# A message-passing layer on one NeuronCore: irregular edge groups moved to a second pass, and another order of TensorE's step

## The reference

```python
h = relu(layernorm(x))
emb = edge_attr_128 @ W_edge + b_edge            # 20000 x 512
msg = relu(h[src] + emb)
h2 = (1 + eps) * h + segment_sum(msg, dst, N)
h2 = gelu(layer_norm(h2 @ W1 + b1, g1, be1))     # 512 -> 1024
h2 = gelu(layer_norm(h2 @ W2 + b2, g2, be2))     # 1024 -> 512
h3 = layer_norm(h + h2, gA, bA)
out = x + layer_norm(h3 + gelu(h3 @ M1) @ M2, gB, bB)
```

## Time and profile before

| quantity | value |
|---|---|
| times of three runs | 535.83, 531.12, 531.4 us; median 531.4 |
| span of the profiled execution | 528.1 us |
| busy PE | 471.7 us, 89% |
| busy PEld | 344.2 us, 65% |
| busy DVE | 393.5 us, 75% |
| busy ACT | 309.2 us, 59% |
| busy POOL | 278.4 us, 53% |
| DMA | 85.53 MB, mean 162 GB/s |

### The profile page before, as it was taken

The page is one execution under the profiler, slowest core; times in us unless marked ns, Lnnn a source line. Parts: engine busy times, 40 slices in busy tenths (PEclk is TensorE's granted clock), DMA queues, the critical chain, the costliest instruction groups (busy, mean ns, idle before and its releaser), DMA issues.

```text
span 528.1 us, 7261 instructions
## 1 busy us (share of the span) xinstructions
PE 471.7 (89%) x1930; PEld 344.2 (65%) x1930; DVE 393.5 (75%) x564; ACT 309.2 (59%) x584; POOL 278.4 (53%) x295
## 2 busy tenths in 40 slices
PE   1397996979996999789987999999999999999994
PEld 0034664646664656446655888888888889888884
DVE  7953995869894889679796577777999866672575
ACT  5643785858874877769793555555666656013000
POOL 5575775767875777667600345533554463330252
PEclk9999998998998999999999999999999999999998
DMA  8956887776786777667604733243551132130122
GB/s 268 345 169 192 305 263 229 231 227 189 248 248 180 207 233 231 185 200 227 188 11 142 260 99 118 82 160 99 159 160 40 61 93 68 40 119 2 41 80 81
DMA packets 31717, 85.53 MB, mean 162 GB/s; under 512 B 4880, under 2 KB 5216, under 8 KB 31648
## 3 DMA queue, kind: packets, MB, share of 16 engines
q0 software_dynamic: 12688, 41.17, 26.7%
q1 hardware_dynamic: 18960, 43.52, 24.7%
HBM read 72.08 MB, written 5.25 MB: 146 GB/s over the span
## 4 chain that ended last, share of the span: by engine, by line
PE 43%; DVE 15%; ACT 14%; issue 11%; ACTq 6%; another core or an unknown queue 3%; POOL 3%; DMA 3%; POOLq 0%; DVEq 0%; SPq 0%
PE ps_u L1288 8%; PE ps_u L1290 8%; PE ps_u L1289 8%; DVE msg_lo L1090 5%; DVE z L1084 5%; ACT apart L690 5%; ACT msg_hi L774 5%; PE ps_t L1290 4%; PE ps_t L1289 4%; PE ps_t L1288 4%; PE ps_t L1462 2%; PE ps_u L1305 2%; DMA w_raw<-in_W 2%; PE ps_t L1323 2%
## 5 line engine op out<-in xcount | busy, mean ns | idle before, releaser
L578 POOL DMA_INDIRECT rows<-gather_table,src_idx x153 | 166.4, 1087 | 66.7 <-issue 43.8
L774 ACT ACTIVATE msg_hi<-z 128x1024 fp32r<-128x1024 f32 (+1 forms) x79 | 82.6, 1046 | 33.4 <-DVE z L1084 22.0
L584 POOL TENSOR_TENSOR var_eps<-mv,eps_t 128x1 f32<-128x1 f32 x40 | 21.5, 536 | 144.0 <-ACT squares L832 85.6
L1090 DVE SCALAR_TENSOR_TENSOR msg_lo<-z,msg_hi 128x1024 fp32r<-128x1024 f32 (+1 forms) x79 | 95.4, 1209 | 0.6 <-ACT msg_hi L774 0.6
L1084 DVE TENSOR_TENSOR z<-ps_u,rows 128x1024 f32<-128x1024 f32 (+1 forms) x53 | 64.3, 1213 | 40.0 <-remote 24.2
L1305 PE MATMUL ps_u<-we_raw,attr_raw 128*128 128x512 f32 x130 | 69.4, 636 | 19.0 <-DVE z L1084 18.4
L1323 PE MATMUL ps_t<-msg_lo,onehot 128*128 128x512 f32 x149 | 64.9, 436 | 2.2 <-ACT onehot L696 1.2
L1288 PE MATMUL ps_u<-w_hi,lhs_lo 128*128 128x512 f32 x160 | 64.5, 403 | 1.5 <-DVE lhs_lo L1132 1.5
L1290 PE MATMUL ps_u<-w_hi,lhs_hi 128*128 128x512 f32 x160 | 62.6, 391 | 0.0
L1289 PE MATMUL ps_u<-w_lo,lhs_hi 128*128 128x512 f32 x160 | 62.3, 389 | 0.0
L1323 PE MATMUL ps_t<-msg_hi,onehot 128*128 128x512 f32 x149 | 59.1, 397 | 0.8 <-issue 0.8
(11 more groups left out here) (179 smaller groups left out, 1015.1 us busy)
## 6 DMA issues: line engine op xcount, KB each, us to landing
attr_raw<-in_attr_t SPq DMA_DIRECT2D x20, 512.0 KB
w_raw<-in_W SPq DMA_DIRECT2D x24, 256.0 KB, 2.8
tile_in<-mid SPq DMA_DIRECT2D x10, 512.0 KB, 3.5
res<-in_x SPq DMA_DIRECT2D x20, 256.0 KB, 2.7
xin<-in_x SPq DMA_DIRECT2D x5, 512.0 KB, 5.6
out<-work SPq DMA_DIRECT2D x10, 256.0 KB, 2.0
rows<-gather_table,src_idx POOLq DMA_INDIRECT x153
gather_table<-tab SPq DMA_DIRECT2D x4, 512.0 KB
```

Source lines behind the costliest of these rows:

```text
L578: g.indirect_dma_start(rows[:, group.r, e % TPG, :], None, gather_table[:, :], bass.IndirectOffsetOnAxis(src_idx[:, e:e + 1].bitcast(u32), ...
L774: a.activation(pair(msg_hi, g, p), summed(g, p), ACT.Relu).then_inc(msg_hi_done, 1)
L1090: v.scalar_tensor_tensor(pair(msg_lo, g, p), summed(g, p), 0.0, pair(msg_hi, g, p).bitcast(f32), ALU.max, ALU.subtract).then_inc(msg_lo_do ...
```

## The change

- **TensorE's step** makes both products first (second pair of g+1, first pair of g+2), then handles an event of group g-1, then scatters both pairs of g-1 with `onehot`, event or not.
- **A plain event** no longer needs a pair with only one window. `old_nodes` scatters into the old window the second pair if bit 4 of the word says that it has edges there, and always the first pair; then TensorE waits for `prefilled` and both pairs are scattered into the new window.
- **Any other event** is a `switch` on ScalarE: close the window before, prefill the group's last one. The group's edges in its last window are scattered as always; those in its other windows are left to a second pass behind the edge stage.
- **The second pass** (`late_windows`) runs on all five engines over all groups, and within a group over the windows left out, one at a time: SyncE loads the attributes, GpSimd gathers the rows, TensorE makes the products, VectorE and ScalarE the messages and a selection, TensorE the sum, VectorE adds it to `acc`. A count in the plan says how many such windows there are; where it is 0 each engine skips the pass. In these inputs it is 0.
- `one_by_one`, `general`, `select_extra` and their tiles and semaphores go; SyncE and GpSimd now wait for the plan before they read the count; the plan's words change.

```diff
-EVENT, COUNTS, SCALAR, LATE, PLAN = 0, 2, 3, 4, 8
+EVENT, SCALAR, LATE, PLAN = 0, 2, 3, 8
...
+        def late_count(engine):
+
+            return field(plan_words(engine, NG, LATE + 2)[0], 0, 9)
+
+        def late_windows(eng, count, body, ready=None):
+
+            with eng.If(count > 0):
+                with eng.Fori(0, NG) as gr:
+                    spans = plan_words(eng.engine, gr, LATE + 1)[0]
+                    lo, extra, before = field(spans, 0, 4), field(spans, 4, 4), field(spans, 8, 9)
+                    with eng.If(extra > 0):
+                        with eng.Fori(1, extra + 1) as k:
+                            body(gr, window(lo + k - 1), before + k)
+                    alone(eng)
+                eng.wait_ge(late_done, count + 1)
...
+            sp.wait_ge(plan_ready, 1)
+            late = late_count(ENG.SP)
             sp.wait_ge(acc_done, 1)
             sp.wait_ge(last_closed, 2)
+
+            def late_attr(gr, w, n):
+                sp.wait_ge(late_done, n)
+                alone(sp)
+                sp.dma_start(attr_raw[:, 0, :], A["attr_t"][:, ds(gr * EG, EG)]).then_inc(late_attr_in, 16)
+
+            late_windows(sp, late, late_attr)
...
+            pool.wait_ge(plan_ready, 1)
+
+            def late_rows(gr, w, n):
+                pool.wait_ge(late_src_ready, n)
+                alone(pool)
+                for e in range(TPG):
+                    g.indirect_dma_start(rows[:, 0, e, :], None, gather_table[:, :],
+                                         bass.IndirectOffsetOnAxis(late_src[:, e:e + 1].bitcast(u32), 0)
+                                         ).then_inc(late_rows_in, 16)
+
+            late_windows(pool, late_count(ENG.Pool), late_rows)
...
-            def prefill(gr):
-
-                spans = plan_words(ENG.Activation, gr, LATE + 2)[0]
-                hi, run = window(field(spans, 0, 4)), field(spans, 4, 9)
-                act.wait_ge(halves_open, 1)
-                act.wait_ge(closed, run)
+            def spans_of(gr):
+                spans = plan_words(ENG.Activation, gr, LATE)[0]
+                return window(field(spans, 0, 4)), window(field(spans, 4, 4)), field(spans, 8, 6)
+
+            def prefill(hi, closes):
+                act.wait_ge(halves_open, 2)
+                act.wait_ge(closed, closes)
                 alone(act)
                 a.activation(ps_t[0][:, ds(bank_of(hi), D)], tile(acc, hi), ACT.Copy).then_inc(prefilled, 1)
 
-            def general(gr):
-
-                spans, counts = plan_words(ENG.Activation, gr, LATE, 2)
-                lo, before, extra = (field(spans, k, 4) for k in (0, 4, 8))
-                extras, number = field(counts, 0, 9), field(counts, 9, 9)
-                act.wait_ge(scattered, gr)
-                alone(act)
-                close(window(before), bank_of(before)).then_inc(closed, 1)
-                with act.If(extra > 0):
-                    with act.Fori(1, extra + 1) as k:
-                        done = window(lo + k - 1)
-                        select_extra(gr, done, number + k)
-                        act.wait_ge(extra_scattered, extras + k)
-                        alone(act)
-                        close(done, bank_of(done)).then_inc(closed, 1)
+            def open_next(gr):
+
+                hi, _, number = spans_of(gr)
+                prefill(hi, number)
+
+            def switch(gr):
+
+                hi, before, number = spans_of(gr)
+                act.wait_ge(halves_open, 2)
+                if not zero(gr):
+                    act.wait_ge(scattered, gr)
+                    alone(act)
+                close(before, bank_of(before)).then_inc(closed, 1)
+                prefill(hi, number + 1)
...
+            def late_high(gr, w, n):
+                act.wait_ge(late_z_done, n)
+                alone(act)
+                a.activation(msg_hi[:, 0, :], z[:, 0:2, :].rearrange("p a d -> p (a d)"), ACT.Relu)
+                for e in range(TPG):
+                    last = a.activation(apart[:, e, :], iota[:, ds(w * P, P)], ACT.Square, bias=neg_dst[:, ds(gr * TPG + e, 1)])
+                last.then_inc(late_apart_done, 1)
+                act.wait_ge(late_apart_done, n)
+                alone(act)
+                a.activation(onehot[0][:, :, :], apart[:, :, :], ACT.Relu, bias=1.0, scale=-2.0).then_inc(late_hi_done, 1)
+
+            late_windows(act, late, late_high)
...
+            v.tensor_tensor(both_f[:, :], later_f[:, :], lo_f, ALU.is_equal)
...
+            onto(word_t[:, :], both_f[:, :], 4, lo_f)
...
+            onto(word_t[:, :], plain_f[:, :], 5, word_t[:, :])
...
+            onto(plan[:, 0:NG, LATE + 1], late_before[:, :], 8, word_l[:, :])
+            onto(plan[:, :, SCALAR], ahead_bits[:, :], 2, word_s[:, :]).then_inc(plan_ready, 1)
...
+            def late_messages(gr, w, n):
+                v.tensor_copy(late_src[:, :], src_idx[:, ds(gr * TPG, TPG)]).then_inc(late_src_ready, 1)
+                dve.wait_ge(late_rows_in, n * (16 * TPG))
+                alone(dve)
+                dve.wait_ge(late_emb_done, n)
+                alone(dve)
+                for p in range(2):
+                    last = v.tensor_tensor(z[:, p, :], ps_u[p][:, :], rows[:, 0, 2 * p:2 * p + 2, :].rearrange("p a d -> p (a d)"), ALU.add)
+                last.then_inc(late_z_done, 1)
+                dve.wait_ge(late_hi_done, n)
+                alone(dve)
+                v.scalar_tensor_tensor(msg_lo[:, 0, :], z[:, 0:2, :].rearrange("p a d -> p (a d)"), 0.0, msg_hi[:, 0, :].bitcast(f32),
+                                       ALU.max, ALU.subtract).then_inc(late_lo_done, 1)
+                dve.wait_ge(late_scattered, n)
+                alone(dve)
+                v.tensor_tensor(tile(acc, w), ps_t[1][:, 0:D], tile(acc, w), ALU.add).then_inc(late_done, 1)
+
+            dve.sem_inc(late_done, 1)
+            late_windows(dve, late, late_messages)
...
-                return t.matmul(summed_in(bank), ident[:, :], tile(acc, w), start=True, stop=True)
+                t.matmul(summed_in(bank), ident[:, :], tile(acc, w), start=True, stop=True).then_inc(halves_open, 1)
...
-            def one_by_one(g, word):
-
-                end = g.tiles - 1
-                counts = plan_words(ENG.PE, g.gr, COUNTS)[0]
-                lo, run = held(field(word, 0, 4), NT - 1), held(field(counts, 0, 9), NG * NT + 1)
-                number, extra = field(counts, 9, 9), field(word, 4, 4)
-                pe.wait_ge(closed, run)
-                alone(pe)
...
-            def two_windows(g, word, bank):
-                number, old = field(word, 10, 6), bank_of(field(word, 0, 4))
+            def old_nodes(g, word):
+
+                old, number = bank_of(field(word, 0, 4)), field(word, 12, 6)
                 pe.wait_ge(first_ready, number + 1)
                 alone(pe)
-
-                def new_open():
-                    pe.wait_ge(prefilled, number)
+                if g.pairs == 2:
+                    with pe.If(word & 1 << 4 > 0):
+                        scatter_first(g, 1, old)
                     alone(pe)
-
-                def both_of_first_pair():
-                    scatter_first(g, 0, old).then_inc(extra_scattered, 1)
-                    new_open()
-                    scatter_last(g, 0, bank)
-
-                if g.pairs == 1:
-                    both_of_first_pair()
-                else:
-                    with pe.If(word & 1 << 8 > 0):
-                        for p in range(2):
-                            last = scatter_first(g, p, old)
-                        last.then_inc(extra_scattered, 1)
-                        new_open()
-                    with pe.Else():
-                        both_of_first_pair()
+                scatter_first(g, 0, old).then_inc(extra_scattered, 1)
+
+            def event(g, word):
+                with pe.If(word > 0):
+                    with pe.If(word & 1 << 5 > 0):
+                        old_nodes(g, word)
+                    pe.wait_ge(prefilled, field(word, 6, 6))
                     alone(pe)
+                alone(pe)
+
+            def words_of(g):
+                word, bank = plan_words(ENG.PE, g.gr, EVENT, 2)
+                return word, nc.s_assert_within(bank, 0, D, skip_runtime_bounds_check_because="the plan has the two halves")
 
             def step(g):
-                before = None if zero(g.gr) else g.next(-1)
-                if before:
-                    word, bank = plan_words(ENG.PE, before.gr, EVENT, 2)
-                    bank = nc.s_assert_within(bank, 0, D, skip_runtime_bounds_check_because="the plan has the two halves")
-                n = g.next(1)
+
+                n, before = g.next(1), None if zero(g.gr) else g.next(-1)
                 if n.gr < NG and n.pairs == 2:
                     embed(n, 1)
-
-                def embed_ahead():
-                    if g.gr + 2 < NG:
-                        embed(g.next(2), 0)
-
-                if before:
-                    with pe.If(word > 0):
```

(94 more changed lines are left out.)

70 lines of the change are left out of this document (22 added, 48 removed).

## The result

The changed kernel took 535.69 us (median of 5 runs, 535.22 to 538.68) against 532.39 us (5 runs) for the kernel before: ratio 1.0081, 95% interval 1.0044 to 1.0119. It is **slower by some 4 us** (3.3 by the medians, 4.3 by the ratio); measured again on three chips it gave 1.0049, 1.0101 and 1.007. The profiled execution spans 533.8 us.

The account below looks back on a forecast made before the run. It took VectorE's stalls before `z`, 39 us of the edge stage, as the loss, blamed on TensorE code fetches. Terms -19.5 + 0 + 3.7 + 0.8 = -15 from 531.4 gave 516 us, range 500 to 534.

Parts of the forecast that it names:

- What bounds the kernel: Edge stage: VectorE loses 39 us in 13 stalls before `z`, waiting for TensorE's late count rather than for rows.
- My reading: Edge stage: while a block of TensorE's code is fetched among the gathers, its counts to other engines are held back.
- TensorE's code: Edge stage: code blocks fall from 24 to about 12, so half the 39 us go: -19.5 us, bounds 0 and -39.
- 142 to 151 us, with more GB/s than 151 to 166 and no stall: Edge-stage windows, 253 against 231 GB/s, cited as evidence against gathers causing the holds.
- The holds follow the gathers, not the code: Rival, 28%: edge-stage holds come with gathers, so shorter code gains nothing: 531 to 536 us, taken 533.
- Order in a step: TensorE's edge-stage step: making both products before both scatters costs nothing: 0 us, bounds -3 and +6.
- The sign that the prediction named: Edge stage: if idle time before `msg_hi` on `scattered` grows, the new order costs; no size given.
- the double product stops ready scatters: Rival, 8%: in edge-stage stalls, scatters are left undone behind the second product; slower by 12 plus 4.5 us: 548 us.
- Events: Edge stage: four plain events make a first-pair last-window scatter skipped before: +3.7 us, bounds 0 and +3.7.
- Second pass: Between edge and dense stages: each engine tests a zero count and skips the pass: +0.8 us, bounds 0 and +3.
- Plan words: VectorE's small plan operations: about as many as before, covered by products needing no plan: 0 us.
- The range: Whole kernel time: 500 to 534 us, leaving out some 2 in 10.

Follow-up runs that it names:

- a_unread: Changed kernel with VectorE adding a fixed SBUF tile instead of gathered rows, not waiting for them; gathers still run: 534.35 us, ratio 1.0016.
- a_nogather: As a_unread, but GpSimd gathers nothing behind group 2: 493.58 us, ratio 0.9254.
- a_hwrows: Changed kernel with SyncE loading neighbouring table rows, the same bytes, in place of GpSimd's gathers: 493.05 us, ratio 0.9244.
- b_hwrows: Kernel before with SyncE loading neighbouring table rows in place of GpSimd's gathers, on a chip without holds: 490.43 us.
- a_narrow_2: As a_unread, all gathers but 512 bytes a row instead of 2048, on a chip with holds: 529.95 us, ratio 1.0029.
- b_short: Kernel before, its order kept, without `one_by_one` and its branch: 531.76 us, ratio 0.9982.
- a_order: Changed kernel with the old order of products and scatters in a step: 534.01 us, ratio 1.0009.
- a_skip4: Changed kernel skipping the first pair's last-window scatter in four plain events, 16 matmuls fewer: 535.90 us, ratio 1.0052.
- a_nolate: Changed kernel without the second pass on any engine: 535.65 us, ratio 1.0063.
- a_half: As a_unread with every second gather left out: 497.42 us on a chip without holds, 496.95 us on one with holds.
- b_lead4: Kernel before with GpSimd at most four pairs ahead of `z` instead of six: 500.61 us, ratio 1.0024, without holds; 526.33 us, 0.9923, with holds.

## Why the prediction failed

**What bounds the kernel** was read rightly in its main step: `z` waits for TensorE's count, not for rows. a_unread shows it, and a_nogather and a_hwrows gain some 40 us, the 39 of the earlier trace rows. Not all of that is waiting for counts. On chip 3, where none is held, taking the gathers away still gave 7.7 us (b_hwrows). And the granted clock is 0.96 in the window of a_unread, 1.00 in those of a_nogather and a_hwrows: in the changed kernel two raw matmuls take 1.29 us behind a pause of 2.41 us, at 147.95, and 1.02 at 140.44. Are the matmuls themselves late, as their ends are modelled? In the stall of the earlier trace rows the trace has the counts of four products and scatters at 86.22, 86.32, 86.38 and 86.44 us, though some 0.9 to 2.5 us of matmuls lie between one and the next. So they had been done, and were let go together. (One count had come through between, at 82.02 us, for a scatter that ended at 75.47; they stay in order.) The Trainium skill ("Perfetto Trace Analysis", section "Tensor Engine Instruction (MATMUL, LD_WEIGHTS)") says that the end in the profile is an estimate and that the count goes out once PSUM has taken the data. A lag of 0.03 us in a_nogather agrees with that estimate.

**The failed step is "My reading"**, and with it the term "TensorE's code", -19.5 us. q8 fell from 24 to 10 (forecast: about 12) and the time did not move. I had a correlation of three windows, one of them without a block or a stall, with two dozen blocks in 228 us, one every 9.5 us: with that many, most stalls have one near them. What the runs show in its place is that the counts are held by GpSimd's gathers: 46.8 us before `z` with all of them and 11 packets of q8, none held with half of them and 13. The row that I set against the rival, "142 to 151 us, with more GB/s than 151 to 166 and no stall", spoke of GB/s, and the gathers hold whatever bytes they move (a_narrow_2). The Trainium skill's "mostly hidden" ("Runtime: NRT & Kernel Launch", section "Instruction fetch mechanics") agrees with b_short, which with 15 blocks for 24 gained nothing that shows.

**The rival "The holds follow the gathers, not the code"**, 28%, is what happened: 533 forecast, 535.69 measured (on a kernel before of 532.39 in place of 531.4). Its mechanism is right, that the size came out so near is partly luck: its terms were the scatters and the pass, of which nothing shows, and what does show is the order, which it had at 0.

**Order in a step**: taken 0, bounds -3 and +6. a_order gives 1.8 us back of the 3.2 (2.4 by the means). The size is within the bounds, the 0 is not borne out. The sign that the prediction named, more idle time before `msg_hi` on `scattered`, is there (13.0 us for 2.3), so the mechanism is likely that of the rival "the double product stops ready scatters", at a fifth of its price of 12 or less.

**Events**: +3.7 with a lower bound of 0 in the shadow of a stall. With the holds in place nothing of it shows (a_skip4 535.90 for 535.85, each known to some 2 us). Without them the change as a whole cost 2.6 us (a_hwrows against b_hwrows, on different chips), where I expected 3.7 to 4.5 (b_hwrows 490.43 for 488.5 to 489.5).

**Second pass**: +0.8. By the profiles 3.62 us from last scatter to dense product instead of 3.14, +0.5; by a_nolate nothing that shows. **Plan words**: nothing of it shows, as forecast; no run tried it alone.

**The range** ended at 534, and the case with 28% stood at 533 with bounds to 536: I cut its upper half. Open are the 1.3 us of 3.2 that no single edit explains (within the intervals), what inside the chip holds a count, and why one chip of five held none: whether that is the chip or something else at that time, no run here separates. The changed kernel did not run with its gathers on that chip.

## What to carry to other kernels

If several engines come loose within 0.1 us of each other, look for one whose only wait is on the suspect (here SyncE's refill) and measure from the end of the work to its start. Before cost is put on what lies near stalls, count how often it lies near none; and try the suspect by taking it away, which here meant dropping a branch that these inputs never take. This kernel, which gathers with GpSimd while TensorE's counts drive the others, took 6 to 7% longer on four chips than on a fifth: compare only on the same chip, and try how far GpSimd should run ahead.

## What the hardware did that I had not expected

- TensorE's counts reach other engines up to 9.05 us late in the trace of before, and 11.94 in that of a_skip4, while GpSimd issues gathers nearly back to back. Of the semaphore records in the trace of before, 40 to 284 us, 65 of 112 of TensorE's came over 0.15 us behind the instruction, one or two of some 160 of ScalarE's and none of 103 of VectorE's.
- The traces with holds also lack records: of the 79 times that `z` raises `z_done`, before has 47 and the changed kernel 44, while a_nogather, a_hwrows, a_half and b_lead4 have them all. The shares above are of the records that are there.
- It isn't in proportion: all gathers cost some 40 us, half of them none; a quarter of the bytes in as many gathers costs about as much as all (529.95 us, 1.0029 of before, for 1.0016 in a_unread).
- The same kernel took 532.6 and 532.7 us on two chips, 528.9 and 527.5 on two and 498.1 on one; kernels without holds agree between chips (a_half 497.42 and 496.95 us).
